# A graph network kernel: carries over three columns a group in six operations of 1024 numbers, a column in front of the ring, gathered rows counted per 16 columns

## Chip, cores and metric

One core of one Trainium2 chip. The metric is the device time of the whole kernel in microseconds, from one launch. POOL is GpSimd, SP is SyncE; POOL issues the indirect DMAs (gathers and scatters by an index column), SP the plain ones.

## The reference

Four graph layers over the same 6250 nodes of 128 features and 106250 edges that are sorted by destination. Each layer normalises the nodes, gathers a row per edge at its source, reduces the rows of each destination (a sum in three of the layers, a maximum in the third, which has four rounds of its own), and adds the result to `x`. Cut to what is gathered and reduced:

```python
# src, dst: 106250 edges, sorted by dst
h = relu(layernorm(x));  x = x + L0(h)   # out[dst] += H[src] * norm
h = relu(layernorm(x));  x = x + L1(h)   # agg[dst] += h[src] * filter(edge_attr) * weight
h = relu(layernorm(x));  x = x + L2(h)   # four times: segment_max over dst of (x[src]-x[dst]) @ tw.T + tb + phi[dst]
h = relu(layernorm(x));  x = x + L3(h)   # two GCN steps: out[dst] += (h @ W)[src] * norm
```

## The kernel before

The edges are padded to 128 x 832 and lie row-wise: partition p holds edges p*832 to p*832 + 831, so a column t is one edge of each partition. Seven times (one step of L0, four rounds of L2, two steps of L3) the function `passing` (L958) runs a pass over the 832 columns: a running sum or maximum along each partition that restarts at each new destination. `layer` (L1126) puts a pass and the update of the nodes behind it into one block of instructions; the last pass stands by itself near the end of the kernel. L1 works with scatters and is not touched.

A pass works in 26 chunks of `WIDE` = 32 columns in the ring `RING_T`, 64 columns of 128 features in the tile `WORK`, so a chunk takes one half of the ring (`RING` = 2).

POOL (`pool_part`) gathers a column at a time: one indirect DMA at L991 takes 128 rows of `table` by the index column `INDEX` (in the tile `S`) into a column of the ring. Ahead of each chunk it waits that the store of the chunk two before is done (`stored`), and ahead of the last gather of a chunk (L990) that VectorE has finished the chunk before (`reduced` against `done`).

VectorE (`dve_part`) works on a chunk in `combine` (L1035), in groups of `FOUR` = 4 columns, 8 groups a chunk. It waits first until all 32 columns have landed (`arrived`, L1026, on semaphores that count 4 columns each, 16 of them for the ring). Then come:

- six operations on 8 x 128 = 1024 numbers, L1045 and L1048 in turn: for j = 1, 2, 3 column j of each group takes in column j - 1, masked by `KEEP` (sum) or `RESET` (maximum). After them each column holds the running value within its group.
- eight `scalar_tensor_tensor` scans of one column, L1053: the last column of each group takes in the last column of the group before, by the mask `PREFIX`. The first of them reads the last column of the chunk before, at the other end of the ring where the chunk is in the first half.
- two operations on 3 x 1024 = 3072 numbers, L1059 and L1064: the three other columns of each group take in the last column of the group before. The first writes the product to `TMP` (in the tile `Z`), the second brings it into the ring. Where the chunk lies in the first half of the ring, each of the two is split in one group (384 numbers) and seven (2688), as the column before the first group lies at the ring's end.

Each VectorE operation counts `reduced` by one and waits for the one before. The last chunk of a pass is done in two: 16 columns by `combine`, and the last 16 one by one by scans at L1074, each as soon as the four columns of its count have landed.

SP (`sp_part`) stores each finished chunk to `run_rows` (L1099), the last one in four parts (16, 8, 6 and 2 columns). When all stores are done POOL gathers the rows at the ends of the destinations from `run_rows` (`run_ends`, L841), and a carry across partitions goes from the last column by way of two transposes on TensorE (L1090, L1092), the tile `carried` (L1086) and an indirect DMA to `carry_rows` (L1001). With these VectorE updates the nodes (L851 on) and the next layer's table is written.

The instructions of an engine run in their order, one at a time. `neutral_value` (0, or -1e38 for a maximum) stands in the ring's last column when a pass begins (L1014).

## Time and profile before

| | |
|---|---|
| median of 3 runs | 10687.7 us (10673.33 to 10689.66) |
| the profiled execution | 10684.92 us, its span 10683.1 us |
| POOL busy | 76% |
| VectorE (DVE) busy | 39% |
| TensorE (PE) busy | 15% |
| DMA engines, mean over the span | 100 GB/s |

The span runs from the first to the last instruction on the slowest (here the only) core. Busy shares are means over the whole span: in the seven passes POOL issues gathers almost without a pause and TensorE does nothing, in the layer with scatters TensorE and ScalarE work as well. In a timeline a row is one instruction, or several of a kind (x8); the brackets tell how long the engine stood idle before it and what ended that. "issue" is time in which the engine waited for nothing that the profile shows. The length of an indirect DMA's row is the time that POOL took to issue it, not that of the transfer.

### The profile page before, as it was taken

The numbers are of one execution on the slowest core, as the hardware profiler recorded it, in microseconds if no ns is written. First come the engines' busy times: TensorE is split into PE (matmuls) and PEld (weight loads), VectorE is DVE, ScalarE is ACT, GpSimd is POOL, SyncE is SP. The second block draws the span as 40 slices with busy tenths as digits, with TensorE's granted clock in tenths as the row PEclk, the third lists the DMA queues.
The fourth block names the chain that finished last, engine by engine and source line by source line (L and its number), as shares of the span: only waits on it lengthen the run. The fifth ranks groups of instructions, "written<-read, shape, count | busy, mean of one in ns | idle before, by whom it ended". The sixth has DMA issues, their size and how long they took to land. (4 is left out here: it accounts for less than half of the span.)

```text
span 10683.1 us, 48143 instructions
## 1 busy us (share of the span) xinstructions
PE 1642.6 (15%) x9025; PEld 1443.0 (14%) x9025; DVE 4206.9 (39%) x7872; ACT 543.4 (5%) x1417; POOL 8083.7 (76%) x7137
## 2 busy tenths in 40 slices
PE   2000048888860000100001000100001000010000
PEld 1000047777750000100001000100001000010000
DVE  4333334444443333333333333333334333433334
ACT  2000021111130000000000000000001000000000
POOL 5777768888847777677776777677777777777777
PEclk7555567677775555555555555555555555555555
DMA  5444435555532222322232222322223222322223
GB/s 186 141 141 142 148 88 77 77 77 77 75 86 87 94 94 94 99 94 94 94 101 92 94 94 94 105 88 94 95 94 99 94 94 94 100 94 94 95 94 107
DMA packets 442216, 1064.84 MB, mean 100 GB/s; under 512 B 153734, under 2 KB 273392, under 8 KB 409786
## 3 DMA queue, kind: packets, MB, share of 16 engines
q0 software_dynamic: 320736, 464.07, 19.5%
q1 hardware_dynamic: 118280, 597.44, 15.2%
q14 instruction: 237, 1.94, 0.1%
q10 hardware_dynamic: 2940, 1.00, 0.0%
q8 instruction: 23, 0.38, 0.0%
HBM read 517.80 MB, written 552.72 MB: 100 GB/s over the span
## 5 line engine op out<-in xcount | busy, mean ns | idle before, releaser
L991 POOL DMA_INDIRECT WORK<-table,S x5824 | 6299.6, 1082 | 2042.5 <-issue 1772.1
L1210 POOL DMA_INDIRECT acc<-TOT,stage x832 | 1301.2, 1564 | 275.0 <-issue 207.1
L1045 DVE TENSOR_TENSOR Z<-WORK,RESET 128x1024 f32<-128x1024 f32 (+1 forms) x312 | 375.8, 1204 | 2789.9 <-DMA WORK<-table,S 2782.8
L1090 PE MATMUL bank<-ident,WORK 128*128 128x128 f32 x7 | 3.3, 474 | 8122.2 <-DVE WORK L1074 8122.2
L1045 DVE TENSOR_TENSOR Z<-WORK,KEEP 128x1024 f32<-128x1024 f32 (+1 forms) x234 | 281.8, 1204 | 2094.1 <-DMA WORK<-table,S 2088.8
L1090 PEld LDWEIGHTS bank<-ident,WORK 128*128 128x128 f32 x7 | 1.3, 181 | 8123.7 <-DVE WORK L1074 8123.7
L1048 DVE TENSOR_TENSOR WORK<-WORK,Z 128x1024 f32<-128x1024 f32 (+1 forms) x546 | 657.5, 1204 | 18.8
L1059 DVE TENSOR_TENSOR Z<-WORK,S 128x384 f32<-128x384 f32 (+3 forms) x273 | 610.2, 2262 | 6.3
L1064 DVE TENSOR_TENSOR WORK<-WORK,Z 128x384 f32<-128x384 f32 (+3 forms) x273 | 606.1, 2247 | 6.3
L1415 DVE SCALAR_TENSOR_TENSOR BASE<-bank,WEIGHT,BASE 128x128 f32<-128x128 f32 x832 | 234.0, 344 | 766.8 <-PE bank L1285 714.1
L1053 DVE SCALAR_TENSOR_TENSOR WORK<-WORK,S 128x128 f32<-128x128 f32 x1428 | 502.5, 352 | 51.1
L1284 PE MATMUL bank<-WF2G,FT 128*128 128x128 f32 x1664 | 420.0, 344 | 0.0
L1285 PE MATMUL bank<-W21Q,ATT 81*128 81x128 f32 x1664 | 415.7, 341 | 0.0
L1295 PE MATMUL bank<-BASE 128*128 128x128 f32 x1664 | 318.2, 352 | 283.3 <-ACT TOT L1344 227.2
L1284 PEld LDWEIGHTS bank<-WF2G,FT 128*128 128x128 f32 x1664 | 350.3, 260 | 0.0
L1285 PEld LDWEIGHTS bank<-W21Q,ATT 81*128 81x128 f32 x1664 | 346.9, 257 | 0.0
L1273 PE MATMUL bank<-ATT,W1Q 81*128 81x128 f32 x1664 | 334.6, 363 | 0.0
L1389 DVE SCALAR_TENSOR_TENSOR BASE<-BASE,KEEP,WORK 128x128 f32<-128x128 f32 x832 | 289.3, 348 | 111.5 <-issue 64.2
L1295 PEld LDWEIGHTS bank<-BASE 128*128 128x128 f32 x1664 | 284.7, 258 | 308.8 <-DVE BASE L1395 164.1
L577 ACT COPY FT<-bank 128x256 f32<-128x256 f32 (+2 forms) x136 | 57.5, 473 | 4892.0 <-PE bank L568 3610.9
L1273 PEld LDWEIGHTS bank<-ATT,W1Q 81*128 81x128 f32 x1664 | 284.3, 258 | 66.2 <-issue 64.5
L841 POOL DMA_INDIRECT NR<-run_rows,idx_max x196 | 199.2, 1017 | 118.6 <-issue 57.0
(247 smaller groups left out, 2654.5 us busy)
## 6 DMA issues: line engine op xcount, KB each, us to landing
run_rows<-WORK SPq DMA_DIRECT2D x175, 2048.0 KB
WORK<-table,S POOLq DMA_INDIRECT x5824
fill_rows<-BASE SPq DMA_DIRECT2D x52, 1024.0 KB
WORK<-fill_rows SPq DMA_DIRECT2D x104, 512.0 KB
table<-TF SPq DMA_DIRECT2D x56, 384.0 KB
WORK<-carry_rows SPq DMA_DIRECT2D x49, 384.0 KB
acc<-TOT,stage POOLq DMA_INDIRECT x832
acc<-Z SPq DMA_DIRECT2D x12, 1024.0 KB
```

The source lines that it names most:

```text
L991: pool.indirect_dma_start(RING_T[:, b * WIDE + k, :], None, table, table_row(table, INDEX[:, t:t + 1]))\
L1045: step(dve.tensor_tensor(TMP[:, 0:groups, 0, :], rows[:, :, j - 1, :], mask(keep[:, :, j], groups, 0), op0))
L1048: step(dve.tensor_tensor(rows[:, :, j, :], rows[:, :, j, :], TMP[:, 0:groups, 0, :], op1))
L1053: step(dve.scalar_tensor_tensor(RING_T[:, last, :], RING_T[:, (last - FOUR) % SPAN, :], prefix[:, g, FOUR - 1:FOUR], RING_T[:, last, :], o ...
L1059: step(dve.tensor_tensor(TMP[:, a:b, :, :], ends.unsqueeze(2).to_broadcast([P, b - a, 3, F]), mask(prefix[:, a:b, 0:3], b - a, 3), op0))
L1064: step(dve.tensor_tensor(rows[:, a:b, 0:3, :], rows[:, a:b, 0:3, :], TMP[:, a:b, :, :], op1))
L1210: pool.indirect_dma_start(acc_dram[a], bass.IndirectOffsetOnAxis(stage[:, h, j % HALF:j % HALF + 1].bitcast(u32), 0), TOT[:, j // QUAD % 2 ...
L1273: m = nc.tensor.matmul(bank(2 + q % 2)[:, j * P:(j + 1) * P], W1Q[:, j, :], ATT[:, q % 4, :], start=True, stop=True)
L1284: nc.tensor.matmul(o, GH[:, q % 2, j * P:(j + 1) * P], WF2G[:], start=True, stop=False)
L1285: m = nc.tensor.matmul(o, ATT[:, q % 4, :], W21Q[:, j, :], start=False, stop=True)
L1295: m = nc.tensor.matmul(bank(1)[:, j * F:(j + 1) * F], SAME[:, q % 4, j, :], MSG[:, q % 2, j, :], start=True, stop=True)
L1389: dve.scalar_tensor_tensor(HX[:, s, :], HX[:, s - 1 if s else 2 * QUAD - 1, :], KEEP[:, ds(t, 1)], FILL[:, h, k, :], ALU.mult, ALU.add)\
```

## The change

- The two operations on 3072 numbers (L1059, L1064) and their splits become six operations on 1024: for each of the three columns j = 0, 1, 2 of all groups one that writes `ends` times (or plus) the mask into `TMP`, and one that brings it into the ring. `TMP` has one column a group in place of three.
- `WORK` is one column longer, and the ring starts a column later. The column in front of it, `BEFORE`, takes the part of the column before the ring's first: it is set to the neutral value at the beginning of a pass, and ahead of each chunk in the first half of the ring, but for the first, a copy of the ring's last column is put there. `ENDS` is the ring seen from `BEFORE` on, so that the last column of the group before is at one stride for all eight groups. `CARRY` begins one column earlier in the ring.
- The landed columns are counted in four semaphores of 16 columns, not in sixteen of 4. `combine` waits for 16 at a time, the scans of L1053 wait for no landing any more, and each of the last 16 columns of a pass waits for the count of all 16.
- POOL's wait ahead of a chunk's last gather: for a chunk in the first half of the ring it still asks for the whole chunk before; for one in the second half only for the copy to `BEFORE`.
- `carried` is a part of `Z` and no tile of its own.

```diff
--- before.py
+++ after.py
@@ -144,10 +144,9 @@
         zeros = Z[:, 0:HALF * F]
         neutral = sb("neutral", [2, F])
         no_node = sb("no_node", [1, BLOCK])
-        WORK = sb("WORK", [P, 4 * HALF * F])
-        RUN = WORK[:, :].rearrange("p (b t f) -> p b t f", b=BUFS, t=HALF)
-        CARRY = WORK[:, 4 * HALF * F - NT * F:].rearrange("p (t f) -> p t f", f=F)
-        FILL = WORK[:, 2 * HALF * F:].rearrange("p (h t f) -> p h t f", h=2, t=HALF)
+        WORK = sb("WORK", [P, (SPAN + 1) * F])
+        CARRY = WORK[:, 4 * HALF * F - NT * F:SPAN * F].rearrange("p (t f) -> p t f", f=F)
+        FILL = WORK[:, 2 * HALF * F:SPAN * F].rearrange("p (h t f) -> p h t f", h=2, t=HALF)
         ACC = WORK[:, 0:2 * ACCS * GROUP * F].rearrange("p (s k t f) -> p s k t f", s=2, k=ACCS, t=GROUP)
 
         def field(k, dt=f32):
@@ -179,7 +178,6 @@
         stage = sb("stage", [P, BUFS, HALF], i32)
         G = Z[:, HALF * F:HALF * F + 8 * F].rearrange("p (a f) -> p a f", f=F)
         carry_t = sb("carry_t", [P, 2, P])
-        carried = sb("carried", [P, F])
         unset = sb("unset", [P, F])
         NR = sb("NR", [P, 2, GROUP, F])
         FE = sb("FE", [P, 2, GROUP, F])
@@ -223,8 +221,11 @@
 
         INDEX = S[:, 0:T].bitcast(i32)
         PREFIX = S[:, T:2 * T]
-        TMP = Z[:, 0:3 * GROUPS * F].rearrange("p (g j f) -> p g j f", g=GROUPS, j=3)
-        RING_T = WORK[:, :].rearrange("p (t f) -> p t f", f=F)
+        TMP = Z[:, 0:GROUPS * F].rearrange("p (g f) -> p g f", g=GROUPS)
+        carried = Z[:, HALF * F:(HALF + 1) * F]
+        RING_T = WORK[:, F:].rearrange("p (t f) -> p t f", f=F)
+        BEFORE = WORK[:, 0:F]
+        ENDS = WORK[:, 0:SPAN * F].rearrange("p (t f) -> p t f", f=F)
 
         banks = [ctx.enter_context(nc.psum_tensor(f"bank{i}", [P, 1024], f32)) for i in range(4)]
 
@@ -269,7 +270,7 @@
         table_out = sem("table_out")
         agg_turned, agg_sb, agg_projected = sem("agg_turned"), sem("agg_sb"), sem("agg_projected")
         carry_in = [sem(f"carry_in{g}") for g in range(NG)]
-        landed = [sem(f"landed{i}", phase=False) for i in range(SPAN // QUAD)]
+        landed = [sem(f"landed{i}", phase=False) for i in range(BUFS)]
         rows_landed = [sem(f"rows_landed{i}", phase=False) for i in range(2)]
         patched = sem("patched", phase=False)
         firsts = sem("firsts", phase=False)
@@ -969,16 +970,13 @@
             parts = (((0, WIDE - HALF),) if WIDE > HALF else ()) + tail
             stored_all = [16 * len(range(b, LAST, RING)) + (16 * len(parts) if LAST % RING == b else 0)
                           for b in range(RING)]
-            steps = 6 + GROUPS + 2
+            steps = 12 + GROUPS
 
             def done(c, n=WIDE):
 
                 if c < LAST:
-                    return (c + 1) * steps + (c + RING - 1) // RING * 2 + (2 if c % RING == 0 else 0)
-                before = done(c - 1)
-                if WIDE > HALF:
-                    before += 6 + HALF // FOUR + 2 + (2 if c % RING == 0 else 0)
-                return before + n - (WIDE - HALF)
+                    return (c + 1) * steps + c // RING
+                return c * steps + (c - 1) // RING + 12 + HALF // FOUR + n - (WIDE - HALF)
 
             def pool_part(pool):
                 for c in range(COUNT):
@@ -987,10 +985,10 @@
                     for k in range(WIDE):
                         t = c * WIDE + k
                         if k == WIDE - 1 and c >= RING - 1:
-                            wait(pool, reduced, done(c - RING + 1))
+                            wait(pool, reduced, done(c - 1) if c % RING == 0 else done(c - 2) + 1 if c > 1 else 0)
                         pool.indirect_dma_start(RING_T[:, b * WIDE + k, :], None, table,
                                                 table_row(table, INDEX[:, t:t + 1]))\
-                            .then_inc(landed[t // QUAD % len(landed)], 16)
+                            .then_inc(landed[t // HALF % BUFS], 16)
                 for b in range(RING):
                     pool.wait_ge(stored[b], stored_all[b])
 
@@ -1011,7 +1009,7 @@
 
             def dve_part(dve, st):
                 dve.memset(unset[:], neutral_value)
-                st.then(dve.memset(RING_T[:, SPAN - 1, :], neutral_value))
+                st.then(dve.memset(BEFORE, neutral_value))
                 if fill:
                     dve.memset(blank, 0.0).then_inc(blanked, 1)
                 if masks is not None:
@@ -1024,44 +1022,41 @@
                     ins.then_inc(reduced, 1)
 
                 def arrived(t):
-                    dve.wait_ge(landed[t // QUAD % len(landed)], base + 16 * QUAD * (t // SPAN + 1))
+                    dve.wait_ge(landed[t // HALF % BUFS], base + 16 * HALF * (t // SPAN + 1))
 
                 def grid(first, groups):
                     return RING_T[:, first:first + FOUR * groups, :].rearrange("p (g j) f -> p g j f", j=FOUR)
 
-                def mask(m, groups, width):
-                    return m.unsqueeze(len(m.shape)).to_broadcast([P, groups, width, F] if width else [P, groups, F])
+                def mask(m, groups):
+                    return m.unsqueeze(2).to_broadcast([P, groups, F])
 
                 def combine(t0, groups):
 
                     first = t0 % SPAN
                     rows = grid(first, groups)
+                    ends = ENDS[:, first:first + FOUR * groups:FOUR, :]
                     keep = scale[:, t0:t0 + FOUR * groups].rearrange("p (g j) -> p g j", j=FOUR)
                     prefix = PREFIX[:, t0:t0 + FOUR * groups].rearrange("p (g j) -> p g j", j=FOUR)
-                    for t in range(t0, t0 + FOUR * groups, QUAD):
+                    if first == 0 and t0:
+                        wait(dve, reduced, n)
+                        step(dve.tensor_copy(BEFORE, RING_T[:, SPAN - 1, :]))
+                    for t in range(t0, t0 + FOUR * groups, HALF):
                         arrived(t)
                     for j in range(1, FOUR):
                         wait(dve, reduced, n)
-                        step(dve.tensor_tensor(TMP[:, 0:groups, 0, :], rows[:, :, j - 1, :],
-                                               mask(keep[:, :, j], groups, 0), op0))
+                        step(dve.tensor_tensor(TMP[:, 0:groups, :], rows[:, :, j - 1, :], mask(keep[:, :, j], groups), op0))
                         wait(dve, reduced, n)
-                        step(dve.tensor_tensor(rows[:, :, j, :], rows[:, :, j, :], TMP[:, 0:groups, 0, :], op1))
+                        step(dve.tensor_tensor(rows[:, :, j, :], rows[:, :, j, :], TMP[:, 0:groups, :], op1))
                     for g in range(groups):
                         last = first + FOUR * g + FOUR - 1
                         wait(dve, reduced, n)
-                        arrived(t0)
-                        step(dve.scalar_tensor_tensor(RING_T[:, last, :], RING_T[:, (last - FOUR) % SPAN, :],
-                                                      prefix[:, g, FOUR - 1:FOUR], RING_T[:, last, :], op0, op1))
-                    wait(dve, reduced, n)
-                    spans = [(0, groups)] if first else [(0, 1), (1, groups)]
-                    for a, b in spans:
-                        ends = RING_T[:, (first + FOUR * a - 1) % SPAN:, :][:, 0:FOUR * (b - a - 1) + 1:FOUR, :]
-                        step(dve.tensor_tensor(TMP[:, a:b, :, :],
-                                               ends.unsqueeze(2).to_broadcast([P, b - a, 3, F]),
-                                               mask(prefix[:, a:b, 0:3], b - a, 3), op0))
-                    wait(dve, reduced, n)
-                    for a, b in spans:
-                        step(dve.tensor_tensor(rows[:, a:b, 0:3, :], rows[:, a:b, 0:3, :], TMP[:, a:b, :, :], op1))
+                        step(dve.scalar_tensor_tensor(RING_T[:, last, :], ends[:, g, :], prefix[:, g, FOUR - 1:FOUR],
+                                                      RING_T[:, last, :], op0, op1))
+                    for j in range(FOUR - 1):
+                        wait(dve, reduced, n)
+                        step(dve.tensor_tensor(TMP[:, 0:groups, :], ends, mask(prefix[:, :, j], groups), op0))
+                        wait(dve, reduced, n)
+                        step(dve.tensor_tensor(rows[:, :, j, :], rows[:, :, j, :], TMP[:, 0:groups, :], op1))
 
                 for c in range(LAST):
                     combine(c * WIDE, GROUPS)
@@ -1130,7 +1125,7 @@
             with nc.Block() as block:
                 update(block, index, base, post, norm_x, weights, finish, before, scatter)
             clear()
-            total.gathers += 16 * QUAD * ROUNDS
+            total.gathers += 16 * HALF * ROUNDS
             total.patches += 32
             for s in range(2):
                 total.rows[s] += 16 * sum(SIZES[s::2])
```

## Rows read from the trace of the kernel before

**Rows 1.** The page: the span, and the busy time of each engine.

```profile
span 10683.1 us, 48143 instructions
...
PE 1642.6 (15%) x9025; PEld 1443.0 (14%) x9025; DVE 4206.9 (39%) x7872; ACT 543.4 (5%) x1417; POOL 8083.7 (76%) x7137
```

**Rows 2.** The page's costliest group: busy us, mean ns, idle before and releaser.

```profile
L991 POOL DMA_INDIRECT WORK<-table,S x5824 | 6299.6, 1082 | 2042.5 <-issue 1772.1
```

**Rows 3.** Waits of POOL: us in total, times, longest us.

```profile
POOL WORK L991 <- issue: 1772.1, 5815, 0.3
```

**Rows 4.** Timeline, a chunk in the ring's second half: start, us, engine, line, operation.

```profile
5060.12 0.94 POOL L991 DMA_INDIRECT WORK<-table,S  x1 [0.30 <-issue]
...
5061.56 1.23 DVE L1045 TENSOR_TENSOR Z<-WORK,RESET 128x1024 f32<-128x1024 f32 x1 [26.30 <-DMA WORK<-table,S]
5062.62 0.99 POOL L991 DMA_INDIRECT WORK<-table,S  x1 [0.30 <-issue]
5062.82 1.22 DVE L1048 TENSOR_TENSOR WORK<-WORK,Z 128x1024 f32<-128x1024 f32 x1
...
5069.12 3.06 DVE L1053 SCALAR_TENSOR_TENSOR WORK<-WORK,S 128x128 f32<-128x128 f32 x8
...
5071.45 0.94 POOL L991 DMA_INDIRECT WORK<-table,S  x1 [0.30 <-issue]
5072.22 3.36 DVE L1059 TENSOR_TENSOR Z<-WORK,S 128x3072 f32<-128x3072 f32 x1
5072.70 3.69 POOL L991 DMA_INDIRECT WORK<-table,S  x1 [0.30 <-issue]
5075.61 3.36 DVE L1064 TENSOR_TENSOR WORK<-WORK,Z 128x3072 f32<-128x3072 f32 x1
5076.69 3.09 POOL L991 DMA_INDIRECT WORK<-table,S  x1 [0.30 <-issue]
```

**Rows 5.** The same timeline, the chunk before it, in the ring's first half.

```profile
5017.68 1.23 DVE L1045 TENSOR_TENSOR Z<-WORK,RESET 128x1024 f32<-128x1024 f32 x1 [27.52 <-DMA WORK<-table,S]
...
5028.33 3.48 DVE L1059 TENSOR_TENSOR Z<-WORK,S 128x384 f32<-128x384 f32 x2
5028.82 0.94 POOL L991 DMA_INDIRECT WORK<-table,S  x1 [0.30 <-issue]
5030.07 2.56 POOL L991 DMA_INDIRECT WORK<-table,S  x1 [0.30 <-issue]
5031.84 3.43 DVE L1064 TENSOR_TENSOR WORK<-WORK,Z 128x384 f32<-128x384 f32 x2
5032.93 3.15 POOL L991 DMA_INDIRECT WORK<-table,S  x1 [0.30 <-issue]
```

**Rows 6.** Groups by line with shapes apart: busy us, mean ns.

```profile
L1059 DVE TENSOR_TENSOR Z<-WORK,S 128x3072 f32<-128x3072 f32 x84 | 282.0, 3357 | 2.9
...
L1059 DVE TENSOR_TENSOR Z<-WORK,S 128x2688 f32<-128x2688 f32 x91 | 272.6, 2995 | 0.0
...
L1048 DVE TENSOR_TENSOR WORK<-WORK,Z 128x512 f32<-128x512 f32 x21 | 14.5, 692 | 0.7
```

**Rows 7.** Timeline of the end of the third pass.

```profile
5582.50 2.51 POOL L991 DMA_INDIRECT WORK<-table,S  x1 [0.30 <-issue]
...
5585.32 1.49 POOL L991 DMA_INDIRECT WORK<-table,S  x1 [0.30 <-issue]
...
5586.02 3.06 DVE L1074 SCALAR_TENSOR_TENSOR WORK<-WORK,RESET 128x128 f32<-128x128 f32 x8
...
5597.21 1.51 DVE L1074 SCALAR_TENSOR_TENSOR WORK<-WORK,RESET 128x128 f32<-128x128 f32 x4 [2.75 <-DMA WORK<-table,S]
...
5601.43 0.94 POOL L841 DMA_INDIRECT NR<-run_rows,idx_max  x1 [5.87 <-DMA run_rows<-WORK]
```

**Rows 8.** Stretches of 2 us behind a store: busy of each engine, PEclk, DMA share, GB/s.

```profile
5036.00:5038.00 2.00, 0.00 (x0) 0.00 (x0) 0.00 (x0) 0.00 (x0) 1.39 (x3) 0.50 0.96 393
...
5042.00:5044.00 2.00, 0.00 (x0) 0.00 (x0) 0.00 (x0) 0.00 (x0) 1.39 (x3) 0.50 0.33 90
```

## The prediction

> **What bounds the kernel now.** The first view to read is the busy table: POOL is busy 8083.7 of 10683.1 us, VectorE 4206.9 [rows 1]. The second is the costliest group, the gathers of L991: 5824 of them, that is 7 passes over 832 columns, 6299.6 us busy [rows 2]. The waits say what POOL waits for between them: nothing but its own issue, 1772.1 us in 5815 waits of at most 0.3 us [rows 3], while VectorE stands idle 26 to 27 us a chunk for gathered rows [rows 4, 5]. No row has a gather waiting for a store or for `reduced`. So in the passes VectorE follows and POOL sets the pace. An undisturbed gather takes 0.94 us and 0.30 us of issue, one each 1.25 us. The mean is 1082 ns instead of 944 [rows 2]: 5824 x 0.138 = about 800 us are lost inside gathers.
>
> The timeline shows where. While the six operations on 1024 numbers run (5061.56 to 5069.1), the gathers stay short (0.99 at the first joint); beside the eight scans (L1053) 0.94; and beside the first operation on 3072 numbers a gather takes 3.69, beside the second 3.09 [rows 4]. Take the operation at 5072.22: it ends at 5075.58, the gather at 76.39, 0.81 later. The next pair: 5075.61 + 3.36 = 5078.97, gather ends 5079.78, again 0.81 later. A gather of 0.94 therefore needs something 0.13 us after its start that a running tensor_tensor holds, and gets it when that operation ends. The gap between the two large operations is only 0.03 us (5075.58 to 5075.61), and the gather gets through it.
>
> The Trainium skill ("SBUF — State Buffer", section "Who interferes with whom") says that a VectorE instruction with two SBUF inputs contends with a GpSimd instruction that reads SBUF. The long rows agree; the eight scans have two SBUF inputs as well, and there the trace shows no stall. Stalls beside scans would stand before and after alike, so the sum is the same by both.
>
> **Part 1: two large operations a chunk become six of 1024.** What it removes, for a chunk in the second half of the ring: the stalls 3.69 + 3.09 - 2 x 0.94 = 4.90 us [rows 4]. In the first half of the ring each large operation is split in 384 + 2688 numbers, and a gather slips in at the joint: 2.56 + 3.15 - 1.88 = 3.83 us [rows 5]. Operations on 3072 come 84 times on L1059, on 2688 91 times [rows 6]: 84 x 4.90 + 91 x 3.83 = 760 us. The last chunk of a pass is done by half, with stalls 2.51 + 1.49 - 1.88 = 2.12 [rows 7], x7 = 15. Together 775 us, the most part of the 800; the rest is what the first six operations cost, and it stays.
>
> What it adds: six operations of 1.22 to 1.23 us, by the same shape now on L1045 and L1048, 0.03 us apart. Their step is 1.26 us (5061.56 to 5062.82) against POOL's own 1.25 [rows 4]. Once a gather has waited for the end of one operation, the next asks 1.25 us later, 0.01 before the next gap. So only the first wait counts, by its phase. In the second half of the ring, the gather of 5072.70 asks at 5072.83, 0.61 us after the run began at 5072.22: it would wait 0.62 for the end of an operation of 1.23 [rows 4]. In the first half the run begins at 5028.33 and the gather of 5028.82 asks at 5028.95: again 0.62 in, so 0.61 of wait [rows 5]. The phase is the same because both runs follow six steps of 1.26 and eight scans (3.06 us) that stay as they are. With 0.05 for five more steps that is 0.67 a chunk, 175 x 0.67 = 117 us. In the half chunk the six operations are of 512 (692 ns, step 0.73) [rows 6]: working the steps through from the gather at 5582.50 gives waits of 0.50, 0.22 and 0.21, 0.93 us, x7 = 7. Saved: 775 - 117 - 7 = 651 us. Bounds: the first wait is between 0 and 1.23 us, so the 117 lie between 9 and 224, and the saving between 544 and 759.
>
> All of it is on the path, since POOL is the pace. VectorE's own time grows from 2 x 3.36 to 6 x 1.26 us a chunk, 0.8 us on some 17.6 in a chunk of 44 (5017.68 to 5061.56) [rows 4, 5]; it hides under the gathers. Of what would come late next: the store of a chunk, issued when VectorE ends at 5035.27, keeps the DMA engines full until 5042 to 5044 [rows 5, 8]; the gathers that write over it start after those of the chunk between, at 5060.12, 16 us later [rows 4], and a chunk shortened to 40.7 us with VectorE 0.8 later takes 4 us of that. The `reduced` wait ahead of a chunk's last gather asks for the chunk before, which VectorE has ended some 20 us earlier. POOL is not slowed by the store (1.39 us busy in the stretch of 2 with the DMA engines full, as much as in the one behind it) [rows 8], so transfers don't become the bound.
>
> The Trainium skill ("VectorE: DVE Perf Modes", section "The TRN2 errata — SBUF-src ops pay a fixed extra latency per instruction") speaks against this part: many small tiles pay a fixed cost each. Here that is the 0.8 us a chunk above, and it would count only if VectorE set the pace.
>
> **Part 2: the column in front of the ring.** One copy of 128 x 128 more on every second chunk, 12 a pass. No row shows it; nearest is a scan of as many numbers, 3.06 / 8 = 0.38 us [rows 4]. It comes 0.03 us after the last operation of a chunk, where VectorE idles for 26 us [rows 4], and POOL asks next 1.25 us after that gap, when the copy is over. I take 0; if it stopped a gather each time it would be 84 x 0.38 = 32 us. Below 0 there is nothing to gain, as it replaces no operation alone. The looser `reduced` wait and `carried` in `Z` change nothing that is waited for.
>
> **Part 3: 16 columns a count.** In a full chunk all 32 columns were waited for before, so nothing moves. The end of a pass is different. There VectorE now scans 8 columns at 5586.02, the next 4 by their own count and, after the last rows land, only 4: 5597.21 to 5598.72 [rows 7]. With one count all 16 start at 5597.21: 15 steps of 0.387 (8 scans in 3.06 us) + 0.35 = 6.1 us, end 5603.3, 4.6 us later. POOL is idle there until the last store lands (gather of L841 at 5601.43, 5.87 idle) and the carry hangs on the same scan, so nothing covers it: 7 x 4.6 = 32 us. Bounds: 0 is excluded, as rows can't be scanned before they are counted; the three last stores now follow each other more closely, at most 1 us each time, so 32 to 39.
>
> **Sum.** Against the profiled execution of 10684.9 us (span 10683.1 and 1.8 around it): - 651 + 32 = - 619, 10066. The median of the runs is 2.8 above, so 10069.
>
> **The rivals.** (a) *The first wait has another phase.* If the run of six started just after a gather's request, the wait would be near 0, 108 us less: 9961; if just before, near 1.23, 107 more: 10176. Against it: both forms of chunk give 0.61 or 0.62. For it: dropped waits could shift the scans a little.
>
> (b) *Slower: POOL misses the 0.03 us gaps.* Then a run of six holds a gather from 0.61 us in to its end, 7.54 - 0.61 = 6.9 us. 175 x 6.9 = 1208 instead of 760: + 448 + 32 = 11168 by the median. It decides against the change once somewhat more than half of that is lost: the gain is gone at 760 + 8 - 32 = 736 us of stalls, where all gaps used give 117 and all missed 1208. Against it: 3.69 ends in the 0.03 gap, and in the first six each gap lets a gather through. The Trainium skill ("SBUF — State Buffer", section "A bandwidth-pool intuition that's wrong (but worth ruling out)") has the blocked DMA go on about 115 ns after VectorE's end, which would be longer than this gap; the trace shows the grant inside the gap.
>
> (c) *No gain: POOL's time is handed to another wait*, for `stored` or `reduced`, and the step of a chunk stays near 44 us: 10688 + 32 = 10720 if all of it is. Against it: the 16 us above. If a part is handed on, the time lies between, and only a narrow band of that is no change.
>
> (d) *The tail is covered* (another chain sets the start of the update): 32 us less, 10037, inside the range.
>
> **How the numbers follow.** Forecast with its phase 0.78, (a) 0.15, (b) 0.03, (c) 0.02, (d) 0.02. The predicted time is 10069. The range takes in both ends of (a) and of the tail: 9960 to 10180. The bound of no change is 0.2% (21 us), about what can be told apart here: faster 0.95 (forecast, a and d), slower 0.04 (b and half of c), same 0.01 (the other half of c).
>
> **What would show it.** Gathers beside the second six: one of about 1.55 us and then 0.95 to 0.97; no gather above 2.5. The group of L991 falls to about 5650 us busy, a mean of 970 ns; a chunk steps in 40.7 us in place of 44 to 45. At the end of a pass 16 scans in one run and the first L841 gather about 8.8 us after that run began (4.2 now). Wrong would be: gathers of over 2 us beside operations of 1024, a gather that waits for a store, or scans that still come in fours.

## The result, and the profile after

The kernel became slower, by 0.3%. It takes 10716.28 us (median of 12 runs, 10708.31 to 10723.39), the kernel before beside it on the same chip 10684.33 (12 runs): ratio 1.0028, 95% interval 1.0021 to 1.0036. The forecast was 10069.

The page of the kernel after, its span, the busy table and the group of the gathers (now L989; busy us, mean ns, idle before and releaser):

```profile
span 10715.3 us, 46813 instructions
...
PE 1637.5 (15%) x9025; PEld 1436.1 (13%) x9025; DVE 4324.5 (40%) x8502; ACT 544.4 (5%) x1417; POOL 7901.4 (74%) x7137
...
L989 POOL DMA_INDIRECT WORK<-table,S x5824 | 6120.3, 1051 | 2103.2 <-issue 1841.5
```

Against [rows 1, 2] POOL is busy 182 us less, the gathers 179 us less, and the span is 32 us longer: what POOL gained, something else took. The waits of the kernel after (us in total, times, longest), four that grew:

```profile
POOL WORK L989 <- issue: 1841.5, 5817, 0.9
...
ACT TF L1178 <- remote: 141.0, 9, 29.8
DVE BASE L1172 <- remote: 112.1, 9, 24.0
...
POOL NR L842 <- DMA run_rows<-WORK: 95.2, 7, 13.7
```

Two of the same view of the kernel before, and its wait for the last store:

```profile
ACT TF L1183 <- remote: 95.6, 9, 16.9
...
DVE BASE L1177 <- remote: 70.6, 9, 12.3
...
POOL NR L841 <- DMA run_rows<-WORK: 41.2, 7, 6.0
```

The longest pause ahead of a gather was 0.3 us [rows 3] and is 0.9 now. POOL's wait for the last store of a pass grew by 95.2 - 41.2 = 54 us in seven passes. "Remote" is a wait at whose end no instruction of another engine ends in the trace: the semaphore step came from elsewhere or came late.

Read from the starts of the gathers, the time splits so. A pass (first gather's start to last gather's end) was 1152 to 1155.5 us and is 1137 to 1138.6: 110.7 us less over the seven. The stretch from a pass's end to the next pass's first gather, the update, was 90.6 to 100.4 and is 116.9 to 120.8; with the one that holds the layer with scatters (1872.1, now 1897.9) that is 135.2 us more, and 8.2 more behind the last pass. The part ahead of the first pass is 0.7 shorter. Together + 32.

**Inside a pass** the forecast held for six chunks and then stopped. A chunk's step in the fourth pass: 40.0, 40.7 five times, 42.0, 44.4, then 44.9 and 44.7 in turn to the end (before: 43.9 and 45.0 in turn). The timeline of the kernel after in its third pass, 14th chunk, around the second six operations (start, us, engine, line):

```profile
5064.17 1.10 POOL L989 DMA_INDIRECT WORK<-table,S  x1 [0.30 <-issue]
5065.57 1.10 POOL L989 DMA_INDIRECT WORK<-table,S  x1 [0.30 <-issue]
5066.46 1.22 DVE L1057 TENSOR_TENSOR Z<-WORK,S 128x1024 f32<-128x1024 f32 x1
5066.97 1.55 POOL L989 DMA_INDIRECT WORK<-table,S  x1 [0.30 <-issue]
...
5068.82 0.95 POOL L989 DMA_INDIRECT WORK<-table,S  x1 [0.30 <-issue]
...
5070.07 0.95 POOL L989 DMA_INDIRECT WORK<-table,S  x1 [0.30 <-issue]
```

One gather of 1.55 and then 0.95: the stalls of over 3 us are gone, as forecast. But the gathers of 1.10, 1.40 us apart, are new; nothing runs on VectorE beside 5064.17 but the scans. New, too, are gathers of 1.94 (at 5057.17) and 1.79 (at 5062.07) beside the first six operations of this chunk, where the kernel before has 0.99 [rows 4]; in the first six chunks of a pass they aren't there.

The rows themselves don't land late. In this pass VectorE starts on a chunk 1.6 to 1.8 us after the chunk's last gather was issued, in the first chunk as in the 25th. So the gathers don't queue up in their transfers.

**Behind a pass** things come late. The kernel after, end of its third pass:

```profile
5594.84 5.00 DVE L1069 SCALAR_TENSOR_TENSOR WORK<-WORK,RESET 128x128 f32<-128x128 f32 x13 [10.04 <-DMA WORK<-table,S]
...
5600.08 0.35 DVE L1069 SCALAR_TENSOR_TENSOR WORK<-WORK,RESET 128x128 f32<-128x128 f32 x1 [0.23 <-DVE WORK L1069]
5601.48 0.35 DVE L1069 SCALAR_TENSOR_TENSOR WORK<-WORK,RESET 128x128 f32<-128x128 f32 x1 [1.05 <-DVE WORK L1069]
5602.88 0.35 DVE L1069 SCALAR_TENSOR_TENSOR WORK<-WORK,RESET 128x128 f32<-128x128 f32 x1 [1.05 <-DVE WORK L1069]
...
5606.72 0.94 POOL L842 DMA_INDIRECT NR<-run_rows,idx_max  x1 [13.59 <-DMA run_rows<-WORK]
```

The last scans wait 1.05 us for nothing but the scan before and start 1.40 apart, the step of the gathers again; POOL is idle for 13.59 where it was 5.87 [rows 7]. Then the update, the first product and its reader on ScalarE and VectorE, after and then before:

```profile
5638.59 0.95 POOL L842 DMA_INDIRECT NR<-run_rows,idx_max  x1 [0.30 <-issue]
5655.43 0.86 ACT L1178 COPY TF<-bank 128x512 f32<-128x512 f32 x2 [29.77 <-remote]
5655.50 1.02 DVE L1172 TENSOR_TENSOR BASE<-bank,bias_e 128x512 f32<-128x512 f32 x2 [23.69 <-remote]
...
5659.25 0.95 POOL L842 DMA_INDIRECT NR<-run_rows,idx_max  x1 [19.71 <-DVE FE L1443]
```

```profile
5619.71 4.61 PE L947 MATMUL bank<-WE,FT 128*128 128x128 f32 x24 [0.95 <-issue]
...
5635.07 0.86 ACT L1183 COPY TF<-bank 128x512 f32<-128x512 f32 x2 [15.42 <-remote]
```

TensorE ends the product at 5630.6 in the kernel after (L948, 24 matmuls from 5625.72, 4.89 us) and ScalarE, which waits for that step alone, reads it 24.8 us later. POOL, VectorE and TensorE work on for a while, POOL's last row there ends at 5639.54 and its transfer at 5640.61; from then on to 5655.43 nothing at all runs. The stretches of the kernel after (busy us of PE, PEld, DVE, ACT, POOL, then PEclk, DMA share, GB/s):

```profile
5641.00:5645.00 4.00, 0.00 (x0) 0.00 (x0) 0.00 (x0) 0.00 (x0) 0.00 (x0) 0.50 0.00 0
5645.00:5649.00 4.00, 0.00 (x0) 0.00 (x0) 0.00 (x0) 0.00 (x0) 0.00 (x0) 0.50 0.00 0
5649.00:5653.00 4.00, 0.00 (x0) 0.00 (x0) 0.00 (x0) 0.00 (x0) 0.00 (x0) 0.50 0.00 0
```

In the kernel before the same step is seen 10.75 us after the product's end (5619.71 + 4.61 = 5624.32 to 5635.07; 8.3 to 12.0 in the second to fourth passes). That, too, is late, and it stood in the trace of before.

### The profile page after: what moved, and what is told of

Its sections match the earlier page's. It is cut to its first block and busy times, and to the rows that moved or that the text cites. A ratio compares the mean times of both kernels' runs of the same rounds, so it can differ in the third digit from the quotient of the medians.

```text
span 10715.3 us, 46813 instructions
## 1 busy us (share of the span) xinstructions
PE 1637.5 (15%) x9025; PEld 1436.1 (13%) x9025; DVE 4324.5 (40%) x8502; ACT 544.4 (5%) x1417; POOL 7901.4 (74%) x7137
## 5 line engine op out<-in xcount | busy, mean ns | idle before, releaser
L989 POOL DMA_INDIRECT WORK<-table,S x5824 | 6120.3, 1051 | 2103.2 <-issue 1841.5
L1049 DVE TENSOR_TENSOR WORK<-WORK,Z 128x1024 f32<-128x1024 f32 (+1 forms) x546 | 659.3, 1208 | 18.8
L1057 DVE TENSOR_TENSOR Z<-WORK,S 128x1024 f32<-128x1024 f32 (+1 forms) x546 | 657.4, 1204 | 18.8
L1059 DVE TENSOR_TENSOR WORK<-WORK,Z 128x1024 f32<-128x1024 f32 (+1 forms) x546 | 657.4, 1204 | 18.8
L1053 DVE SCALAR_TENSOR_TENSOR WORK<-WORK,S 128x128 f32<-128x128 f32 x1428 | 503.7, 353 | 50.7
L842 POOL DMA_INDIRECT NR<-run_rows,idx_max x196 | 199.6, 1018 | 204.4 <-DVE FE L1443 70.7
L1384 DVE SCALAR_TENSOR_TENSOR BASE<-BASE,KEEP,WORK 128x128 f32<-128x128 f32 x832 | 289.3, 348 | 39.2 <-DMA WORK<-fill_rows 36.4
```

What stands on the lines that cost most here:

```text
L842: pool.indirect_dma_start(NR[:, g % 2, t, :], None, run_rows, table_row(run_rows, index[:, k:k + 1])).then_inc(rows_landed[g % 2], 16)
L989: pool.indirect_dma_start(RING_T[:, b * WIDE + k, :], None, table, table_row(table, INDEX[:, t:t + 1]))\
L1049: step(dve.tensor_tensor(rows[:, :, j, :], rows[:, :, j, :], TMP[:, 0:groups, :], op1))
L1053: step(dve.scalar_tensor_tensor(RING_T[:, last, :], ends[:, g, :], prefix[:, g, FOUR - 1:FOUR], RING_T[:, last, :], op0, op1))
L1057: step(dve.tensor_tensor(TMP[:, 0:groups, :], ends, mask(prefix[:, :, j], groups), op0))
L1059: step(dve.tensor_tensor(rows[:, :, j, :], rows[:, :, j, :], TMP[:, 0:groups, :], op1))
```

## The experiments

The theories at first: A, POOL's indirect DMAs have a limit of their own, and what a pass gains under it comes back behind it; B, the counts of 16 columns are the cause. Two kernels take the change apart. The edits are cut to the lines that matter; the counts and waits that follow from them are left out. A ratio is always to the kernel before on the same chip, whose median lies between 10676 and 10695 from chip to chip. The kernel after with the counts of 4 columns again (quad_six):

```diff
-        landed = [sem(f"landed{i}", phase=False) for i in range(BUFS)]
+        landed = [sem(f"landed{i}", phase=False) for i in range(SPAN // QUAD)]
```

> The changed kernel with its landed rows counted per 4 columns again: the six operations and the column in front of the ring stay. In the changed kernel six chunks of a pass step in 40.7 us, as forecast, and from the eighth on they step in 44.8, with gathers of 1.10 us and pauses of 0.86. Theory A (something beside the shared hold limits the gathers to about 1.40 us each over a longer time, and a reserve of some 27 us lets a pass begin faster): passes stay at about 1137 us, chunks at 44.6 to 45.0 from the eighth on; the scans at a pass's end come in fours again and 7 x 4.6 = 32 us come back: 10680 to 10690. Theory B (the coarser count itself slows the gathers or the semaphores): chunks step in 40.7 to the end of a pass, passes of 1060 us, about 10050 in all.

Measured: 10713.32 us, ratio 1.0035 (1.0023 to 1.0048). Passes 1138, updates 115 to 120, chunks 40.8 and from the eighth 44.8. The coarse counts aren't the cause. But the 32 us that theory A wanted back (10680 to 10690) didn't come either: with the scans in fours again the kernel is no faster than the kernel after (1.0028).

The reverse, the kernel before with counts of 16 (half_two):

```diff
-                            .then_inc(landed[t // QUAD % len(landed)], 16)
+                            .then_inc(landed[t // HALF % BUFS], 16)
```

> The kernel before with its landed rows counted per 16 columns: the two large operations stay. Theory A: chunks step in 43.9 and 45.0 as before and passes take 1153 us; only the 16 scans at the end of a pass add 7 x 4.6 = 32 us: 10710 to 10725. Theory B: gathers of 1.10 us and pauses of 0.86 appear here too, passes get longer than 1160 us, over 10750 in all.

Measured: 10694.75, ratio 1.0016 (1.0006 to 1.0026), 18 us more, where 10710 to 10725 was expected. Its last rows of a pass, scanned in one run, and the first gather of the run ends:

```profile
5596.89 6.16 DVE L1073 SCALAR_TENSOR_TENSOR WORK<-WORK,RESET 128x128 f32<-128x128 f32 x16 [11.22 <-DMA WORK<-table,S]
...
5605.76 0.94 POOL L841 DMA_INDIRECT NR<-run_rows,idx_max  x1 [10.52 <-DMA run_rows<-WORK]
```

16 scans at 0.387 us, and POOL idle for 10.52 where it was 5.87: 4.65 us, Part 3's 4.6. Of 7 x 4.65 = 33 us, 18 are seen in the whole.

Is the step of 1.40 VectorE's doing? quad_six without the twelve `tensor_tensor` of a chunk (scans_only):

```diff
-            steps = 12 + GROUPS
+            steps = GROUPS
...
-                    for j in range(1, FOUR):
...
-                    for j in range(FOUR - 1):
```

> The kernel of quad_six with all twelve tensor_tensor operations of each chunk left out, so that VectorE does only the eight scans: the sums are not formed, nothing holds a gather up. Theory A: the first five or six chunks of a pass step in 40.0 us, later ones in 44.8 again, a pass of about 1130 us. Theory C (the limit comes from how gathers and the twelve operations fall together): 40.0 us a chunk to the end, passes of about 1040 us.

Measured (one run): 10702.94, the kernel before 10676.3. With 26.3 us of VectorE work left in 400 (3900 to 4300), chunks take 40.0 at first and 44.8 from the eighth on, and the gathers are 1.400 apart, one after the other. Its timeline where the step changes:

```profile
4979.44 0.94 POOL L989 DMA_INDIRECT WORK<-table,S  x1 [0.30 <-issue]
4980.69 0.95 POOL L989 DMA_INDIRECT WORK<-table,S  x1 [0.30 <-issue]
4981.94 1.05 POOL L989 DMA_INDIRECT WORK<-table,S  x1 [0.30 <-issue]
4983.30 1.09 POOL L989 DMA_INDIRECT WORK<-table,S  x1 [0.30 <-issue]
4984.70 1.09 POOL L989 DMA_INDIRECT WORK<-table,S  x1 [0.30 <-issue]
4986.10 1.09 POOL L989 DMA_INDIRECT WORK<-table,S  x1 [0.30 <-issue]
```

So VectorE's work doesn't limit POOL (the other engines do none in a pass), and stalls that are removed leave the step at 1.400. From here theory E: POOL can issue one indirect DMA per 1.400 us for long; a reserve lets it run ahead at 1.25; while it is ahead, other engines' semaphore steps are seen late, up to all that is owed. In the kernel after the reserve is the saving of the first eight chunks against 44.8: 4.8 + 5 x 4.1 + 2.8 + 0.4 = 28.5 us.

Two kernels hold POOL back in each chunk, so that it never runs ahead (paced11, paced12):

```diff
+                        if k == 12 and c >= 1:
+                            pool.wait_ge(reduced, done(c - 1))
```

> The kernel of quad_six with one wait more: ahead of a chunk's twelfth gather POOL waits until VectorE has done the chunk before, so the average pace falls below the limit seen. Theory E (gathers drain at 1.40 us each through something with a reserve of some 28 us; while that is full, VectorE's and TensorE's semaphore steps are late as well): chunks step in about 45.8 us to the end, no gather of 1.10 us and no scan step of 1.40; at the end of a pass nothing is left to drain, so the first product of an update is taken up by ScalarE within 2 us (22 to 31 us late in quad_six), and an update is 85 to 90 us long in place of 118. All: 7 x 1187 + 7 x 88 and the rest, 10680 to 10740. Theory F (the late steps of the update come from the new code and not from the gathers' pace): updates stay at 118 us, over 10900.

> The same wait one gather later, for a step of about 44.6 us, just inside the limit of 44.8. Theory E: passes of about 1157 us, updates of 85 to 95 us, 10600 to 10680 in all, faster than the kernel before if the updates lose their late steps. Theory F: updates of 118 us, 10700 to 10750.

Measured: paced11 10979.07, ratio 1.0277 (1.026 to 1.0294), paced12 10755.49, ratio 1.007 (1.0053 to 1.0086). Both miss theory E's times by far, and paced11 even lies where rival F put it. The updates decide: 91 to 99 us in both, where F asked for 118. The chunks step in 46.2 and 44.9 us, a little more than planned, and the sum for paced11 was wrong in itself: its passes and updates with the layer with scatters (1869.5) and both ends (254.2) make some 10870. paced12, timeline at the added wait:

```profile
5098.47 1.56 POOL L991 DMA_INDIRECT WORK<-table,S  x1 [0.30 <-issue]
5100.34 0.95 POOL L991 DMA_INDIRECT WORK<-table,S  x1 [0.31 <-issue]
5105.77 0.94 POOL L991 DMA_INDIRECT WORK<-table,S  x1 [4.49 <-DVE WORK L1044]
5107.02 0.95 POOL L991 DMA_INDIRECT WORK<-table,S  x1 [0.30 <-issue]
```

In paced12 20 gathers take 1.08 to 1.12 us (15 in the kernel before, 968 in the kernel after), no scan steps at 1.40, and each of the 175 full chunks has one gather of about 1.55. I had looked for updates of 85 to 95, so part of their length is the update's own. ScalarE sees the first product 6.4 to 7.1 us after TensorE's end in paced12 and 4.0 to 10.6 in paced11, not within 2 as E had it, but far from the 24.8 to 25.3 of the kernel after. And the group of the gathers of paced12 is the one that the prediction had drawn:

```profile
L991 POOL DMA_INDIRECT WORK<-table,S x5824 | 5648.6, 970 | 2773.4 <-issue 1718.6
```

Does idle time fill the reserve again? One hold of some 20 us ahead of the 17th chunk (pause):

```diff
+                        if k == 0 and c == 16:
+                            pool.wait_ge(reduced, done(c - 1))
```

> The kernel of quad_six with POOL held once a pass, ahead of the first gather of chunk 16, until VectorE has done chunk 15, some 20 us. Theory E: the reserve fills by those 20 us, so about five of the chunks behind it step in 40.7 again before 44.8 comes back, and the whole takes as long as quad_six, within 20 us. Theory G (the fast chunks belong to the beginning of a pass, by code or cold tables): chunks step in 44.8 behind the pause too, and the whole takes 7 x 20 = 140 us more.

Measured (one run): 10714.98, the passes 1138 us as without the hold. The timeline at it:

```profile
3907.04 0.94 POOL L991 DMA_INDIRECT WORK<-table,S  x1 [20.73 <-DVE WORK L1044]
3908.29 0.94 POOL L991 DMA_INDIRECT WORK<-table,S  x1 [0.30 <-issue]
...
3949.51 1.06 POOL L991 DMA_INDIRECT WORK<-table,S  x1 [0.30 <-issue]
```

The chunks behind it take 40.0, 40.8 three times and 41.5, then 44.7: 4.8 + 12.0 + 3.3 = 20.1 us under 44.8, for 20.73 of idle. Idle time costs nothing here, and it comes back whole.

What is counted? Half as many rows in a gather from the third chunk on (rows64), and eight more plain DMAs of 64 KB a chunk by SP (extra_dma), both on scans_only:

```diff
+                        w = P if c < RING else P // 2
```

```diff
+                        for i in range(8):
+                            a = (c * 8 + i) * F
+                            sp.dma_start(spare[:, a:a + F], unset[:]).then_inc(extra, 16)
```

> The kernel of scans_only with gathers of 64 rows in place of 128 from the third chunk of each pass on; half of the rows keep what was there, the sums are not formed. Theory H (what drains counts rows or their descriptors): no limit shows, as 64 rows would need 0.70 us; chunks step in POOL's own time for 64 rows, at most 40.0 us, to the end. Theory I (it counts DMAs or their semaphore increments, the same 16 each): 44.8 us a chunk as before, or 1.40 us a gather.

> The kernel of scans_only (no tensor_tensor operation in the chunks, sums not formed) with eight more DMAs of 64 KB on SP's queue behind each store. Theory J (what drains counts every DMA): 40 DMAs a chunk at 1.40 us, chunks of 56 us once the reserve is used. Theory K (POOL's gathers alone): 44.8 us as in scans_only. Between them, 45 to 55: other DMAs count with another price.

Measured (one run each): 10711.01 and 10710.98. Both go back to 44.8 a chunk. Between 3900 and 4300 the DMA share is 0.30 in scans_only, 0.22 with half the rows and 0.34 with the added DMAs, and POOL issues 286 or 287 gathers in all three: neither rows, bytes nor SP's DMAs count. That the stores of a chunk hold the gathers up has no test of its own: a kernel with all but two columns of each store left out (small_store) gave no time.

If the number of gathers counts, leaving some out must pay 1.400 us each (fewer, on quad_six):

```diff
+                        if c >= RING and k % 8 == 7:
+                            continue
```

> This is quad_six with every eighth column's gather left out from the third chunk of each pass on (28 gathers a chunk instead of 32; the rows of the columns left out aren't fetched, so this part of the computation is missing); everything else of a chunk, its six sums on 1024 numbers twice, its scans and its stores, stays. Theory E (gathers can't be issued for long at more than one per 1.400 us): a chunk of 28 gathers takes 28 x 1.25 + 0.7 = 35.7 us while the reserve lasts and 28 x 1.400 = 39.2 us after it; a pass with the product behind it is shorter by 96 x 1.400 = 134 us, 7 passes by 940 us, so about 9775 us in all. Rival T (the limit is one of time per chunk, or of something else in the chunk than its gathers, such as its semaphore steps on the other engines): chunks go back to 44.8 us with 28 gathers of 1.60 us each, and the whole stays within 30 us of 10713.

Measured (one run): 9768.22, forecast 9775. Its page's group of gathers:

```profile
L991 POOL DMA_INDIRECT WORK<-table,S x5152 | 5339.7, 1036 | 1950.6 <-issue 1684.1
```

Chunks of 28 gathers take 35.7 at first and 39.2 in the limit, 28 x 1.400; pass and update together take 1116.5 to 1124.1 us instead of quad_six's 1252.7 to 1257.9. Theory E stands in the passes; a limit of time per chunk falls. (What goes with a gather, its instructions on POOL and its count of a semaphore, is left out with it.)

Can the reserve be used without being exhausted? The six operations only in the first four or six chunks, two large ones in the others (mix4, mix6):

```diff
+                    if t0 // WIDE < 4:
```

> The kernel of quad_six with the six operations only for the first four chunks of a pass; the other chunks use two operations on 3072 numbers, unsplit, as the column in front of the ring allows. Theory E: four chunks step in 40.7, the others in 45.0, just over the limit of 44.8, so by the end of a pass 16 to 19 us are owed in place of 28 in quad_six: no gather of 1.10, no scan step of 1.40. Passes of about 1149 us. If an update is late only where the reserve is near its end, it takes 98 to 102 us: 10640 to 10675, a little faster than the kernel before. If it is late in step with what is owed: 103 to 108 us, 10680 to 10710.

> The same with six chunks in place of four. Theory E: passes of about 1141 us, 24 to 26 us owed at their end, just inside the reserve. Updates of 98 to 104 us if only a full backlog makes them late, 10590 to 10640; 112 to 117 us if they are late in step with what is owed, 10690 to 10720.

Measured: 10723.38, ratio 1.0026 (1.0017 to 1.0036), and 10722.1, ratio 1.0026 (1.0016 to 1.0036). Passes of 1151.5 and 1144.5, updates of about 106 and 113 us, ScalarE's first copy 19 and 26 us after TensorE's end. So the steps are late in step with what is owed, and nothing is kept; both times are above the expected ones, on a chip whose kernel before takes 10695.37.

half_two with the last 16 columns of a pass on counts of 4 (tail_four):

```diff
+                    if t >= T - HALF:
+                        dve.wait_ge(last_landed[t // QUAD % len(last_landed)], 16 * QUAD * (passes + 1))
+                        return
```

> This is half_two (the kernel before with counts of 16 columns), but the last 16 columns of a pass keep their four counts of 4. half_two's passes were 1150 to 1153 us long where those of the kernel before are 1152 to 1155.5, and its first gather of the run ends came 4.7 us later, behind 16 scans in one run. Expected by both theories: the scans of the end come in 8, 4 and 4 again and the first gather of the run ends is back at 5.9 us after the pass's last gather. Theory E (what a pass gains comes back in the update as long as POOL is near its bound of one gather per 1.400 us): passes 1150 to 1151, the stretch from a pass's end to the next pass's start longer by as much, 92 to 102 us, and the whole within 0.1% of the kernel before (ratio 0.999 to 1.001). Rival F (at 1.388 us a gather POOL is not at the bound, and the gain is kept): 2 to 2.5 us a pass less with updates as before, 14 to 18 us in all: ratio 0.9983 to 0.9987, a version a little faster than both.

Measured: 10678.83, ratio 0.9997 (0.9988 to 1.0006). The tail is as before (8, 4 and 4 scans), and so are the passes, 1152 to 1155.5: the gain over which E and F differ didn't come, so this tells nothing of E. It does tell that the whole of half_two's 18 us was the coarse count of the last 16 columns. This kernel is no faster than the one before, and no other that was tried and does the whole work is.

Last, whether the changed ring makes the limit: the kernel before, less its eight `tensor_tensor` of a chunk (before_scans):

```diff
-            steps = 6 + GROUPS + 2
+            steps = GROUPS
```

> The kernel before, without the six operations on 1024 and the two on 3072 numbers of a chunk (that part of the computation is missing); the eight scans, the gathers, the stores and the counts of 4 columns stay, and the ring lies as before, with no column in front of it and no copy. Until now the bound of 1.400 us a gather was seen only in kernels with the changed ring. In all of those (after, quad_six, scans_only, pause, rows64, extra_dma, mix4, mix6) ScalarE's first product of the update starts 1199.4 to 1199.8 us after the pass began; in the kernel before it starts at 1191.6. Theory E (the bound belongs to POOL's indirect DMAs, whatever the ring): chunks 40.0 at first, 44.8 from the eighth on, passes 1137 to 1138, first product at 1199.5, 10690 to 10715 us in all. Rival L (the changed layout makes each gather dearer, and with the old ring the bound is lower): first product at 1191.6 or earlier, chunks of 44.5 us or less from the eighth on, whole at least 50 us shorter, 10640 or less.

Measured (one run): 10708.38, the kernel before 10683.26. Chunks of 40.0 and from the eighth on 44.8, passes 1137.7 to 1139.2, first product 1199.3 us after the pass's start. The old ring has the same limit; rival L falls. Mark what this run says: with most of VectorE's work in the passes taken away, and with all large operations gone, the kernel before is no faster.

One table holds the argument, read in the third pass of each kernel (us; "first product" is the start of ScalarE's first copy in the update):

| kernel | pass | pass's end to first product | sum | pass's end to next pass |
|---|---|---|---|---|
| before | 1152.1 | 39.5 | 1191.6 | 100.4 |
| half_two | 1151.2 | 41.8 | 1193.0 | 100.7 |
| tail_four | 1152.1 | 36.6 | 1188.7 | 95.5 |
| paced12 | 1164.7 | 36.3 | 1201.0 | 97.6 |
| mix4 | 1151.5 | 48.4 | 1199.9 | 109.6 |
| mix6 | 1144.5 | 55.1 | 1199.6 | 111.9 |
| after | 1137.1 | 62.3 | 1199.4 | 119.5 |
| scans_only | 1137.8 | 61.6 | 1199.4 | 117.3 |
| before_scans | 1137.7 | 61.6 | 1199.3 | 120.3 |
| fewer | 1003.5 | 61.7 | 1065.2 | 118.8 |

In scans_only TensorE ends that product 28.8 us after the pass, in the kernel after 37.5 and in fewer 43.0, and ScalarE sees it 61.6 to 62.3 us after it all the same. From mix4 down to before_scans the sum is 1199.3 to 1199.9, however the pass was spent: up to the first product POOL has issued 832 gathers, 24 of L842 (L841 in before_scans) and one scatter of the carry, and 857 x 1.400 = 1199.8. fewer has 96 less, 134.2 us less, 1.398 each. The second and fourth passes give the same within 1 us, and the fifth, with 859 to 863 indirect DMAs, 1205 to 1209. The sixth doesn't fit: 857 of them, and 1192.1 in the kernel after, 1185.2 in scans_only.

## Why the prediction was wrong

**What bounds the kernel: wrong, and this is the step that failed.** "So in the passes VectorE follows and POOL sets the pace. An undisturbed gather takes 0.94 us and 0.30 us of issue, one each 1.25 us." The rows are right and the conclusion isn't: 1.25 is the step of a POOL that has a reserve, 1.400 the one it can hold. With the stalls, the kernel before made one gather per 1152.1 / 832 = 1.385 us. Of the 800 us of stalls the passes lost only 111; the rest stood in place of a wait that comes without them. The trace of before shows no pass without stalls, so it has no row at 1.40; but it has semaphore steps that ScalarE sees 8.3 to 12.0 us after TensorE made them, and I didn't read them, because they lie behind the passes.

**Part 1, the sizes: right, the saving: wrong.** One gather of 1.55 us and then 0.95, and 40.7 us a chunk, for six chunks of a pass, where 40.7 was forecast. Forecast for all: 5650 us busy and a mean of 970 ns; measured 6120 and 1051. Where POOL is kept under its limit the forecast sizes are all there: 5648.6 us and 970 ns in paced12, 5645.5 and 969 in paced11. Instead of 651 us the passes gave 110.7, and the reserve is what bounds that: 28.5 us a pass, of which the kernel before had already used 832 x 1.400 - 1152.1 = 12.7; 7 x (28.5 - 12.7) = 111 (this adds up measured chunks; nothing ahead of the run would have told the 28.5). "All of it is on the path, since POOL is the pace" fails a second time behind the pass: the 110.7 came back as 135.2 + 8.2 us, of which 54 are POOL's longer wait for the last store.

**Part 2: right.** 0 was the forecast. The copy takes 0.23 us, and beside the first three copies of a pass, where POOL isn't limited yet, the gather takes 0.95 or 0.96, as an undisturbed one does. Later it takes 1.10, as its neighbours do.

**Part 3: the mechanism right, the price half, and nothing beside the six operations.** half_two has the tail 4.65 us longer (forecast 4.6), and 18 us of the 32 in the whole; tail_four gives them back. In the kernel after the tail itself grew by 7.7 us (5.87 to 13.59), 3 us more than by counts alone, since its last scans step at 1.40. But quad_six has the fours again and isn't faster (1.0035 against 1.0028): when the first product comes 1199.4 us after the pass's start in any case, the tail isn't on the path.

**The rivals.** (c) gives 10720 for 10716, but by luck: it let a gather wait for `stored` or `reduced`, and no such wait is in the waits of the kernel after. What it had right is its form, that POOL's saved time is handed to another wait. I gave it 0.02, because I searched for that wait among the kernel's own semaphores. (b) fell: every gap of 0.03 us lets a gather through.

**What stays open.** What the limit of 1.400 us is made of; the runs say only that it counts POOL's indirect DMAs, or what goes with each of them, and not their rows, bytes, or SP's DMAs. The Trainium skill ("NOTIFIC — the notification-queue block", section "7.1 Overflow: three behaviours, one of which stalls the engine") has a block that records events and can hold an engine back when it falls behind; that could look like this, and no run here shows it. Every time on record comes with a recorded span, so whether the limit is there without the recording is open as well. Open too is why the kernel before, half_two and tail_four reach their first product 6.5 to 11 us sooner than the 1199.5 of all the limited kernels, mix4 among them, whose pass is as long: its step is seen 19.4 us late, that of tail_four 7.7. A single rate of 1.400 with a reserve doesn't give that difference, nor the sixth pass. And that late steps make up the longer updates rests on their size and on the paced kernels; no experiment took the lateness alone away.

## What to carry to other kernels

An engine that issues without a pause has not shown its sustained rate as long as something else stalls it: before pricing stalls at their full length, take the stalling work out in one throwaway kernel and see whether the engine gets faster at all (before_scans, scans_only: for seven chunks of a pass, and not in the whole). Look for late semaphore steps, waits on a producer that ended long ago, also in stretches far from the change; they are the sign of a resource that is already behind. On such a kernel leaving out DMAs of that queue pays, here 1.40 us for each gather; of what was tried, nothing else did.

## What the hardware showed that was not expected

- POOL's indirect DMAs settle at one per 1.400 us (44.8 us for 32, 39.2 for 28), with 128 rows or 64. Ahead of that some 28 us can be had at 1.25, and idle time pays them back one to one (20.73 for 20.1).
- While POOL is ahead, a semaphore step between two other engines can be seen 25 to 33 us after the instruction that makes it ended (24.8 in the kernel after, 32.8 in scans_only), the last 14.8 us of it, in the kernel after, with no engine and no DMA at work; and single instructions of VectorE that wait for the one before can start 1.40 apart (two steps at the end of each pass in the kernel after). The gathered rows aren't seen late meanwhile (1.6 to 1.8 us).
- A gather beside a chain of operations on 1024 numbers is held once (1.55 us) and then slips through gaps of 0.03 us (175 chunks of 175 in paced12; once POOL is at its limit there are others of 1.79 and 1.94).
